# Attention and routed experts on one core: the experts' scale and shift made once, one product for the output's shift, and routing and projection steps in other places of the hand-written slots

## The reference

```python
x = x + attention(layernorm(x))       # 16 heads, causal mask, softmax
z = layernorm(x)
probs = softmax(z @ Wr + br)          # 8 experts
topw, topi = top_k(probs, 2); topw /= sum(topw)
def expert(z, Wi, bi, Wg, bg, Wo, bo, g, b):
    h = gelu(z @ Wi + bi) * sigmoid(z @ Wg + bg)       # 512 wide
    r = z + (h @ Wo + bo)
    return (r - mean(r)) * rsqrt(var(r) + 1e-12) * g + b
x = x + sum of topw * expert(z) over the token's 2 experts
```

## Time and profile before

| | before |
|---|---|
| median of 3 runs | 1237.73 us |
| the profiled execution | 1241.94 us, with a span of 1240.2 us |
| TensorE busy | 1105.6 us, 89% of the span |
| VectorE busy | 982.0 us, 79% |
| ScalarE busy | 796.9 us, 64% |
| GpSimd busy | 741.8 us, 60% |
| attention at full pace | from 98 to 735 us |
| experts | from 813 to 1191 us |
| last stage | from 1191 to 1240 us |

### The profile page before, as it was taken

One profiled execution on the slowest core, in us unless ns is written; L12 is line 12 of the kernel. 1 busy time (PEld: TensorE's weight loads), 2 busy tenths in 40 slices (PEclk: granted clock), 3 DMA queues, 4 the chain that ended last, 5 costly groups with the idle time before them and its releaser, 6 DMA issues. The chain is left out here.

```text
span 1240.2 us, 27505 instructions
## 1 busy us (share of the span) xinstructions
PE 1105.6 (89%) x8654; PEld 835.8 (67%) x8654; DVE 982.0 (79%) x2792; ACT 796.9 (64%) x1800; POOL 741.8 (60%) x1359
## 2 busy tenths in 40 slices
PE   3899999999999999999999998179999999999930
PEld 1565655665656666666666664079999999999920
DVE  4777778788788788788878873758888888888859
ACT  2465665675666666666666565268888888888810
POOL 2257475675576576576576566716666666666640
PEclk9999999999999999999999998579999999999975
DMA  5223545434434434433433421521111111111138
GB/s 145 94 77 113 168 135 166 130 93 125 130 101 125 129 109 123 131 105 113 142 112 93 138 60 36 171 53 53 52 53 54 53 53 53 53 53 53 32 123 305
DMA packets 138270, 127.38 MB, mean 103 GB/s; under 512 B 71848, under 2 KB 96432, under 8 KB 138128
## 3 DMA queue, kind: packets, MB, share of 16 engines
q1 hardware_dynamic: 127184, 103.59, 28.7%
q0 software_dynamic: 8640, 17.84, 4.4%
q10 hardware_dynamic: 2304, 4.20, 0.9%
HBM read 71.13 MB, written 54.43 MB: 101 GB/s over the span
## 5 line engine op out<-in xcount | busy, mean ns | idle before, releaser
L808 ACT ACTIVATE probs<-st 128x384 f32<-128x384 f32 (+1 forms) x768 | 389.1, 525 | 204.9 <-PE st L704 181.8
L849 DVE TENSOR_REDUCE neg_max<-sa 128x2 fp32r<-128x1024 f32 (+3 forms) x384 | 395.6, 1036 | 135.1 <-PE sa L689 126.9
L642 POOL TENSOR_SCALAR_AFFINE_SELECT probs<-probs 128x128 f32<-128x128 f32 (+1 forms) x768 | 245.5, 332 | 243.1 <-ACT probs L808 232.6
L704 PE MATMUL st<-q_stack,k_pad 128*128 128x256 f32 (+2 forms) x1024 | 338.4, 372 | 15.6 <-DMA q_stack<-max_scratch 9.1
L684 PE MATMUL sa<-k_pad,q_stack 128*128 128x256 f32 (+2 forms) x1024 | 328.1, 363 | 12.8 <-DVE neg_max L849 6.7
L684 PEld LDWEIGHTS sa<-k_pad,q_stack 128*128 128x128 f32 x1024 | 178.0, 192 | 111.8 <-issue 69.8
L704 PEld LDWEIGHTS st<-q_stack,k_pad 128*128 128x128 f32 x1024 | 177.2, 192 | 48.4 <-ACT probs L808 20.9
L1006 POOL DMA_INDIRECT y_scratch<-z,to_row x142 | 170.7, 1202 | 35.9 <-issue 35.9
L1040 PE MATMUL up<-xt_hi,w_cur 128*128 128x256 f32 x568 | 167.7, 295 | 0.0
L717 PE MATMUL pv<-probs,v_aug 128*32 128x512 f32 (+3 forms) x2048 | 167.1, 445 | 0.0
L1041 PE MATMUL up<-xt_lo,w_cur 128*128 128x256 f32 x568 | 161.6, 285 | 0.0
(11 more groups left out here) (160 smaller groups left out, 1477.2 us busy)
## 6 DMA issues: line engine op xcount, KB each, us to landing
q_stack<-q_scratch SPq DMA_DIRECT2D x64, 256.0 KB, 2.6
k_pad<-k_scratch SPq DMA_DIRECT2D x256, 64.0 KB, 2.5
xg<-rows_scratch SPq DMA_DIRECT2D x71, 130.0 KB
q_scratch<-q_hi SPq DMA_DIRECT2D x16, 512.0 KB, 3.1
k_scratch<-k_hi SPq DMA_DIRECT2D x16, 512.0 KB, 2.9
y<-y_scratch SPq DMA_DIRECT2D x16, 512.0 KB, 5.3
q_scratch<-q_lo SPq DMA_DIRECT2D x17, 256.0 KB, 3.1
k_scratch<-k_lo SPq DMA_DIRECT2D x17, 256.0 KB, 3.1
```

The source lines that it names most:

```text
L642: pool.affine_select(out=blk, in_=blk, compare_op=ALU.is_ge, fill=0.0, base=0, pattern=[[0, w], [1, P]], channel_multiplier=-1).then_inc(m ...
L704: last = nc.tensor.matmul(st[:, t % 2, at:at + w], k_pad[:, G * g + j, kk * P:(kk + 1) * P], q_stack[:, g, S - w:S], start=True, stop=True)
L808: nc.scalar.activation(probs[:, n % 2, j, lo:lo + w], st[:, k % 2, at:at + w], ACT.Exp).then_inc(exp_done, 1)
L849: V.tensor_reduce(neg_max[:, n % 2, heads[0]:heads[-1] + 1, i], scores[:, :, 0:(i + 1) * P], AX.X, ALU.max, negate=True).then_inc(sa_read, 1)
```

## The change

In the experts the scale and shift of all 8 experts are laid into an SBUF tile `gb_sb` once, by four steps `GBa` to `GBd` in the tail of attention (two products on TensorE and one copy of 128x512 on ScalarE each). The step `gamma_beta` of each block and the waits on it are taken out, and `scale` and `shift` read `gb_sb`. The two products L1051 of each block become one of 256 columns, over both halves, which now lie in one PSUM tile.

In attention the order inside the slots is another, shown in full below. `V` goes from slot 0 to slot 1 and out of `FIRST`; `Rc` from slot 0 to slot 3; `Rf` from slot 1 to slot 0; `Ra` and `LGa` lie before `a4` of slot 2; `zn` goes from slot 2 to slot 1; `out` and `ln2` to the start of slot 1; `xT`, `Q`, `K`, `Kl` and `ST` to earlier places of slot 3.

```diff
         SLOT = {
-            0: "SR A0 B0 a0 B1 PV0 A1 B2 a1 B3 mT mE A2 B4 mW a2 B5 Rc A3 V B6 a3 B7 A4 B8 Rd PV1 PV2 PV3 a4 OT CM B9 mR AR XL A5 B10 RC a5 Re B11 ON",
-            1: "SR A0 B0 a0 Rf B1 PV0 A1 B2 out a1 B3 mT mE A2 S0 B4 mW a2 B5 A3 S1 B6 a3 B7 ln2 A4 B8 S2 PV1 PV2 PV3 a4 OT B9 mR rs2 A5 B10 RC a5 B11 ON",
-            2: "SR A0 B0 a0 ln B1 zn PV0 S3 A1 B2 a1 B3 mT mE rs1 A2 B4 mW a2 B5 zT A3 S4 B6 a3 B7 A4 LG B8 xn PV1 PV2 PV3 a4 OT B9 mR A5 B10 RC LGa a5 B11 ON",
-            3: "SR A0 Ra B0 a0 B1 PV0 S5 A1 B2 a1 B3 mT mE A2 EX S6 B4 mW a2 B5 xT A3 Rb S7 B6 a3 B7 Q A4 B8 Ql PV1 PV2 PV3 a4 OT K B9 mR A5 B10 RC a5 B11 Kl ST ON",
+            0: "SR A0 B0 a0 Rd B1 PV0 A1 B2 a1 B3 CM mT mE A2 B4 mW a2 B5 A3 B6 a3 B7 A4 B8 Re Rf PV1 PV2 PV3 a4 OT B9 mR AR XL A5 B10 RC a5 B11 ON",
+            1: "SR A0 B0 out a0 ln2 B1 PV0 S0 A1 B2 a1 B3 mT mE rs2 A2 S1 B4 mW a2 B5 V A3 S2 B6 a3 B7 A4 B8 zn PV1 PV2 PV3 a4 OT B9 mR A5 B10 RC a5 B11 ON",
+            2: "SR A0 B0 zT a0 ln B1 PV0 S3 A1 B2 a1 B3 mT mE rs1 A2 S4 B4 mW a2 B5 LG A3 B6 a3 B7 A4 B8 LGa Ra xn PV1 PV2 PV3 a4 OT B9 mR A5 B10 RC a5 B11 ON",
+            3: "SR A0 B0 EX xT a0 Rb B1 PV0 S5 A1 B2 a1 Q B3 mT mE A2 S6 B4 mW a2 Ql B5 A3 K S7 B6 a3 B7 Kl A4 B8 Rc PV1 PV2 PV3 a4 OT B9 mR ST A5 B10 RC a5 B11 ON",
         }
-                    "Ra": -1, "EX": -1, "Rb": -1, "Rc": -2, "Rd": -2, "CM": -2, "Re": -2, "Rf": -2, "S": -2}
-        FIRST = "ln rs1 xn xT Q Ql K Kl ST SR0 SR1 SR2 SR3 V"
+                    "Ra": -1, "EX": -1, "Rb": -1, "Rc": -1, "Rd": -2, "CM": -2, "Re": -2, "Rf": -2, "S": -2}
+        FIRST = "ln rs1 xn xT Q Ql K Kl ST SR0 SR1 SR2 SR3"
...
-        LAST = """PD BU AR Rc- Rd- CM- Re- Rf- W0 W1 W2 out ln2 S0- rs2 zn S1- W3 W4 W5 W6 zT W7 W8 LG LGa S2- S3- Ra EX
+        LAST = """PD BU GBa GBb GBc GBd AR Rd- CM- Re- Rf- W0 W1 W2 out ln2 S0- rs2 zn S1- W3 W4 W5 W6 zT W7 W8 LG LGa S2- S3- Ra EX
...
+                elif kind in GB_STEPS:
+                    misc_free(pe, kind, n)
+                    pe.wait_ge(r_const, made["b_stack, b_sel"])
+                    for half in range(2):
+                        e = 2 * GB_STEPS.index(kind) + half
+                        last = nc.tensor.matmul(misc[:, half * 2 * D:(half + 1) * 2 * D], b_sel[:, e * P:(e + 1) * P],
+                                                b_stack[:, D:3 * D], start=True, stop=True)
+                    last.then_inc(misc_written, 1)
...
+                if kind in GB_STEPS:
+                    i = GB_STEPS.index(kind)
+                    act.wait_ge(misc_written, misc_use(kind, n))
+                    act.wait_ge(pv_written, GROUPS_ALL)
+                    nc.scalar.activation(gb_sb[:, i * 4 * D:(i + 1) * 4 * D], misc[:, :], ACT.Copy).then_inc(gb_done, 1)
...
+                nc.tensor.matmul(y_ps[:, :, :], b_sel[:, bass.ds(e * P, P)],
+                                 b_stack[:, 0:D].unsqueeze(1).broadcast_to([P, 2, D]), start=True, stop=True)
                 for h in range(2):
-                    nc.tensor.matmul(y_ps[h][:, :], b_sel[:, bass.ds(e * P, P)], b_stack[:, 0:D],
-                                     start=True, stop=False)
                     for c in range(FC):
-                        last = nc.tensor.matmul(y_ps[h][:, :], hid[:, u % 2, c, h * P:(h + 1) * P],
+                        last = nc.tensor.matmul(y_ps[:, h, :], hid[:, u % 2, c, h * P:(h + 1) * P],
                                                 wo_sb[:, bass.ds(e * (FC * D) + c * D, D)],
-                                                start=False, stop=(c == FC - 1))
+                                                start=False, stop=True, skip_group_check=True)
                 last.then_inc(y_written, 1)
 
-            def gamma_beta(s, u):
-                e = expert_of(u)
-                if not before(s, 1):
-                    pe.wait_ge(z_done, s)
-                nc.tensor.matmul(gb_ps, b_sel[:, bass.ds(e * P, P)], b_stack[:, D:3 * D],
-                                 start=True, stop=True).then_inc(gb_written, 1)
...
-                                                  gb_ps[:, 0:D], ALU.subtract, ALU.mult)
+                                                  gb_sb[:, bass.ds(e * (2 * D), D)], ALU.subtract, ALU.mult)
...
-                                                  gb_ps[:, D:2 * D], ALU.mult, ALU.add)
+                                                  gb_sb[:, bass.ds(e * (2 * D) + D, D)], ALU.mult, ALU.add)
```

More of the change, by code:

```diff
@@ L184, in attention_and_routed_experts @@
         w_hi_done, w_lo_done = sem("w_hi_done"), sem("w_lo_done")
+        gb_done = sem("gb_done")
         pads_made, runs_done, pads_stored = sem("pads_made"), sem("runs_done"), sem("pads_stored")
@@ L238, in attention_and_routed_experts @@
         ORDER, TAIL = list(schedule()), list(tail())
-        MISC_USERS = ("xT", "Q", "K", "V", "zT", "LG", "CM", "BU")
+        GB_STEPS = ("GBa", "GBb", "GBc", "GBd")
+        MISC_USERS = ("xT", "Q", "K", "V", "zT", "LG", "CM", "BU") + GB_STEPS
         MISC_ORDER = [(kind, n) for kind, _, n in ORDER + TAIL if kind in MISC_USERS]
@@ L396, in misc_free @@
                                "V": (vaug_done, b_ + 1), "zT": (zT_done, b_ + 1), "LG": (logits_done, b_ + 1),
-                               "CM": (rank_done, b_ + 1), "BU": (b_up_done, 1)}[before]
+                               "CM": (rank_done, b_ + 1), "BU": (b_up_done, 1),
+                               **{step: (gb_done, i + 1) for i, step in enumerate(GB_STEPS)}}[before]
                 pe.wait_ge(done, count)
@@ L441, in attention_and_routed_experts @@
         wo_sb = sb("wo_sb", [P, E * FC * D])
+        gb_sb = sb("gb_sb", [P, E * 2 * D])
         route = part = ExitStack()
@@ L625, in constants @@
                                                             base=0, pattern=[[-1, E], [0, P]], channel_multiplier=1))
+                    made["b_stack, b_sel"] = count["const"]
             for kind, k, n in ORDER:
@@ L933, in attention_and_routed_experts @@
         up = pb("up", [P, 4, F])
-        y_ps = [pb(f"y_ps{h}", [P, D]) for h in range(2)]
+        y_ps = pb("y_ps", [P, 2, D])
         xt_ps = pb("xt_ps", [P, BR])
-        gb_ps = misc[:, 0:2 * D]
         gathered = [sem(f"gathered{u}") for u in range(NX)]
@@ L942, in attention_and_routed_experts @@
         up_written, up_read = sem("up_written"), sem("up_read")
-        hid_done, gb_written = sem("hid_done"), sem("gb_written")
+        hid_done = sem("hid_done")
         y_written, res_done, ve_done, dev_done = sem("y_written"), sem("res_done"), sem("ve_done"), sem("dev_done")
@@ L1141, in residual @@
                 for h in range(2):
-                    last = V.scalar_tensor_tensor(res[:, u % NR, h, :], y_ps[h][:, :], 0.5, xg[:, u, h, 0:D],
+                    last = V.scalar_tensor_tensor(res[:, u % NR, h, :], y_ps[:, h, :], 0.5, xg[:, u, h, 0:D],
                                                   ALU.mult, ALU.add)
```

9 lines of the change are left out of this document (4 added, 5 removed).

## The result

The change makes the kernel slower by 0.6%: 1245.57 us against 1237.27 us for the kernel before (medians of 9 runs each; 1241.91 to 1249.05 and 1235.57 to 1242.25), a ratio of 1.0062 with a 95% interval of 1.0042 to 1.0082. The forecast was 1235 us, no change. The time lies in the wide range of 1214 to 1250, but outside 1229 to 1241, the range of the sum as it stands, and the change has the sign to which I gave 0.24.

A forecast was written before the change was run, and what follows sets the result against it. TensorE was taken to bound the kernel, busy throughout the experts and for 637 of 655 us in attention. Experts -8, attention +5 and tail 0 gave -3 us: 1239 against the profiled execution, 1235 against the median, range 1214 to 1250.

The forecast's parts named there:

- the sum as it stands: Whole kernel: the added-up terms hold, 1229 to 1241 us, chance 0.45.
- the sign to which I gave 0.24: Whole kernel: slower, above 1243.9 us, chance 0.24; faster had 0.36 and within 0.40.
- the sum for attention: Attention: -22 us of waits that go and +28 that come, +6 by terms, +3 by slots, taken as +5.
- the term (1): Slot 3: `K` waits behind `Ql` on VectorE, TensorE stands 1.25 us, +17 us in 14 sequences (0 to 20).
- Term (2): Slot 1: `ln2` ahead of `a1` waits for `out`, so `A3` waits 0.7 us, +10 us in 14 sequences (0 to +18).
- The waits for maxima and exponentials: Attention: moved VectorE steps give -7 us (-12 to 0), `zn` moved to slot 1 gives -4 us (-6 to 0).
- The load of the maxima: Slot 1: with `K`, `Kl` and `ST` earlier, TensorE's wait for this load goes whole, -11 us (-9.1 to -12.8).
- the tail: End of attention: four `GB` steps of 1.1 us each delay `CM` but lose nothing, 0 us (0 to +2).
- A counted wait isn't there: Attention: one or both added waits are absent: 1225 without (2), 1218 without (1), 1208 us without both; chance 0.27.
- VectorE late in slot 3: Slot 3: `Rc` and `Kl` ahead of `a4` make VectorE late and the next `A0` wait: 1249 us, chance 0.17.
- The experts give nothing: Experts: the merged product runs slower or L1063's place was filled with latency: 1243 us, chance 0.08.
- GpSimd and VectorE meet: Experts: `scale` and `shift` with two SBUF tensors and GpSimd's power block each other, +34 us, 1270 us; chance 0.03.

The follow-up runs named there:

- The run with `K` later: The changed kernel with `K` moved behind `A4` and `Kl` behind `B8` in slot 3: 1234.13 us, ratio 0.9958 to the kernel before.
- The experts' part alone: The kernel before with only the experts' changes (`GBa` to `GBd`, `gb_sb`, merged product) and its old slot order: 1224.07 us, ratio 0.9879.
- the merge alone: The kernel before with only the two L1051 products of each block made one of 256 columns, L1063 kept: 1231.16 us, ratio 0.9936.
- the slots' part alone: The kernel before with only the four new slot lists, its experts unchanged: 1262.12 us, ratio 1.0187.
- the selector step earlier: The changed kernel with GpSimd's `SU3` moved from the second slot of sequence 1 to the last slot of sequence 0: 1239.58 us, ratio 1.0012.
- the kernel with the sum earlier: The changed kernel with `K` behind `A4`, `SU3` one sequence earlier, `out` at the end of slot 0 and `ln2` behind `a0`: 1216.79 us, ratio 0.9835.
- the two fastest runs: The changed kernel with `K` behind `A4`, `SU3` earlier, and either `ln2` behind `a2` (1220.51 us) or `out` at the end of slot 0 (1216.79 us).
- the statistics three steps later: The changed kernel with `ln2` of slot 1 moved behind the maximum of `a2` and `rs2` behind `A3`: 1240.21 us, ratio 1.0007.

## Why the forecast was wrong

**The sign came from attention.** Forecast was +5 us there and -8 us among the experts. By the runs with one part each, attention is +23.7 and the experts' part -14.4. The step that failed is the sum for attention, and within it these terms:

- *Slot 3, forecast 13.1, measured 13.89: 0.8 x 14 = 11 us.* The wait of `K`, the term (1), was forecast at 1.25 us and is 1.0 in the waits, or 1.4 from where `K` would be due if `B5` had not been late; its chain, 2.0 to 2.2 us by the forecast, takes 2.17. So this term holds to 0.2 us, and the other 0.6 us a sequence lie in what I had laid around it. No run splits them up. The run with `K` later, which has no `misc` wait, still needs 12.80 us where the kernel before has 12.00, and two causes are read in it: `B5` waits for the exponential behind `q_hi` (some 0.4 us against the same step in slot 0), and the next `A0` waits 0.3 us for VectorE, fuller by `Rc` and `Kl`. I costed `Q`'s new place at nothing, for TensorE; its ScalarE half met the exponentials.
- *A wait once, 6.7 us (18.2 against 11.5).* Term (2) priced the chain `out` to `ln2` to `A3` with the typical start of `out`. I did not look for the slots in which GpSimd has extra work ahead of it; `SU3` is in the list, and its move alone gave 6.0 us.
- *The waits for maxima and exponentials, forecast -7 and -4.* I took them from the waits of the weight loads, 17.4 and 12.0 us. The products themselves waited only 3.7 and 1.2 us in that trace, so there was less to gain than I took. In the trace after the weight loads wait 20.0 and 12.8 us.
- *The load of the maxima, forecast -11.* It went from the trace, but it is a wait that differs between executions. The experts' part alone, with the same slots as before, shows 5.0 us in 7 waits, and the merge alone 6.7 us in 8, where the profile that I had shows 9.1 in 10. Here is the row of the experts' part alone:

```profile
PE st L709 <- DMA q_stack<-max_scratch: 5.0, 7, 1.6
```

  In both the last four slots begin 4.1 us earlier (at 731.1) than in the profiled execution before, which is 4 us above the median that I had. I subtracted the 4 us from the whole time and left them in the gain, so they were counted twice.
- *The last four slots, forecast 0, measured -5.5 between the two traces.* Not forecast at all. The early `ln2`, which I priced only at `A3`, shortens the waits for exponentials here, and the clock falls less: 0.86 before, 1.00 after. How much falls to the clock is luck of the execution in part. With the same last lists the slots' part alone takes 31.0 us at 1.00, and the selector step earlier and `K` behind `A4` take 33.4 at 0.90; with the old lists the experts' part alone takes 36.4 at 0.91.

**Right, within 0.1 us.** Slot 0 (10.2 forecast, 10.15), slot 2 (11.05, 11.08), the typical slot 1 (11.6, 11.5), with `A3`'s wait of 0.7 (0.7 to 0.8); no row that waits for `q_stack<-max_scratch` in this trace (the slots' part alone has one, of 1.3 us); the tail, +0.5 us in a forecast of 0 to +2. A `GB` step takes 1.30 us and not 1.1, and VectorE idles 3.74 us for `CM`; but its operation ends 7.4 us behind the last `pv` (794.46 - 787.06), and in the kernel before 7.3 (778.91 by the earlier trace rows, less 771.59), where it ended with GpSimd's memset.

**The experts: mechanism right, size wrong.** L1063 was forecast at 0.11 us, and is 0.114. The merge was forecast at 0 ±2 and is -0.108 x 71 = -7.7 us: this is the mis-sized term. I took the price by columns, with "one record's fixed cost" as the far bound of ±0.03; a record among float32 products costs about 0.11 us whether it has 128 or 256 columns here, and the earlier trace rows with 0.116 us a record, the value I used for L1063, would have pointed to it. The 5.18 us of a block is 290 us over 56 blocks, of which the window holds parts; from block to block it was 5.21. The rule on VectorE's price in the Trainium skill (VectorE: DVE Perf Modes, The TRN2 errata) is not what this kernel shows: by it the two steps on `gb_sb` gain, and they went from 342 to 350 and from 329 to 349 ns.

**The rivals.** *A counted wait isn't there* (0.27) is false for both, they are there. *VectorE late in slot 3* (0.17) is close in its time, 1249 against 1245.6, but not in its mechanism: no `A0` waits for the maxima behind slot 3 in the kernel after; it appears with 0.3 us only when `Kl` is moved too. *The experts give nothing* (0.08) is false, *GpSimd and VectorE meet* (0.03) too: its power takes 1079 ns (L1017) against 1070 before, and VectorE idles for `gate`. The two steps on `gb_sb` were hardly put to it, since only 1 of their 284 runs beside the power. `hid`, with two SBUF tensors, does in 138 of 142, and takes 689 ns there and 692 otherwise.

**The books.** Forecast against the median -2.7 us; experts -7.7; slot 3 +11; the one wait +6.7; the last slots -5.5; the double count +4; the tail +0.5. That gives +6.3, against +8.3 measured (+5.2 to +10.1 by the interval). These terms are read between two traces, and none of them holds the 3.7 us by which the trace after lies below its median; with them it is +10.0. So the books close to 2 us, and not better.

**Open.** The kernel after varies by 7 us between executions and the kernel with the sum earlier by 1.5. The long slots of sequences 1 to 3 move from trace to trace (15.6 in one, 11.8 in another), and the loads issued beside them are the likely reason. No run left those loads out. The clock moves with it: the four slowest of the nine executions after (1247.16 to 1249.05) have a mean granted clock of 0.956 to 0.958, the five fastest 0.959 to 0.960. Which of the two is the cause of the other is not settled.

## What to carry to other kernels

A step that is moved has a half on every engine that takes part in it: list what stands behind each half in that engine's queue, for the typical pass and for the passes with extra work. Take the gain from a wait that differs between executions from the level to which you will compare, not from a profile that is a slow one. Look at the granted clock of each stretch before a difference is put down to the order of the steps: the last four slots took 31.0 or 33.4 us with the same lists, at 1.00 and at 0.90, and they, not the typical slot, made the difference between the two fastest runs. And a reader should stand well behind the writer on another engine: with the sum one slot earlier, as with the statistics three steps later, `A3` had no wait, but the later statistics made everything behind them late.
